# Strassen's block products for the up projections of a gated block on one Trainium2 core

## What is computed

```python
x = x + tanh(g_xattn[0]) * wkv(time_decay, time_first, k=layernorm(x), v=ctx_2048)
n = layernorm(x)
up_gate = einsum('bsd,hd->bsh', n, W1)      # W1, W3: 2048 x 512
up_lin  = einsum('bsd,hd->bsh', n, W3)
hidden  = fwht(silu(up_gate) * up_lin)      # Walsh-Hadamard along 2048, over sqrt(2048)
x = x + tanh(g_ffn[0]) * einsum('bsh,dh->bsd', hidden, W2)
```

## Time and profile before

| | us |
|---|---|
| median of 3 runs (range) | 1097.14 (1094.07 to 1098.11) |
| profiled execution | 1094.78 |
| its span, first to last instruction | 1093.0 |
| PE busy | 1060.4 |
| DVE, ACT, POOL busy | 585.2, 306.8, 290.7 |
| one steady run, from one store of the output to the next | 127.76 |
| mean granted TensorE clock | 0.997 |

### The profile page before, as it was taken

How to read it: one execution, slowest core, us unless ns; L and a number is a source line. 1 busy time by engine, 2 the same in 40 slices (tenths; PEclk the granted TensorE clock), 3 DMA queues, 4 the chain that set the end, 5 groups by cost and what they waited for, 6 DMA issues and landing times.

```text
span 1093.0 us, 12943 instructions
## 1 busy us (share of the span) xinstructions
PE 1060.4 (97%) x4878; PEld 498.6 (46%) x4972; DVE 585.2 (54%) x841; ACT 306.8 (28%) x377; POOL 290.7 (27%) x198
## 2 busy tenths in 40 slices
PE   5798999999999999999999999999999999999998
PEld 2365444444444444444444444444444444444443
DVE  7857986475284644665554752746436645531112
ACT  6756511413123311324113131143113241100000
POOL 0131152124321252223421244122521234211111
PEclk9899999999999999999999999999999999999999
DMA  9943030001200020001100012000200000000001
GB/s 351 345 182 130 1 116 1 40 1 38 77 1 40 24 93 1 3 39 39 77 1 39 1 39 77 3 39 7 109 1 1 39 1 1 1 39 1 1 1 39
DMA packets 19955, 55.65 MB, mean 51 GB/s; under 512 B 1072, under 2 KB 10416, under 8 KB 17072
## 3 DMA queue, kind: packets, MB, share of 16 engines
q1 hardware_dynamic: 19888, 54.73, 13.9%
HBM read 42.14 MB, written 12.58 MB: 50 GB/s over the span
## 4 chain that ended last, share of the span: by engine, by line
PE 90%; DVE 4%; ACT 2%; DMA 2%; issue 1%; SPq 1%; POOL 0%; DVEq 0%; ACTq 0%
PE pg L470 10%; PE po L478 10%; PE pl L470 10%; PE pg L468 10%; PE po L476 10%; PE pl L468 10%; PE pl L469 9%; PE po L477 9%; PE pg L469 9%; PE pst L403 1%; PE po L451 1%; DMA w_turn<-x 1%; DMA x<-w_t 1%; PE pst L434 1%; PE pst L439 1%
## 5 line engine op out<-in xcount | busy, mean ns | idle before, releaser
L1065 POOL TENSOR_TENSOR work<-work 128x512 bf16<-128x512 f32 (+1 forms) x132 | 202.4, 1533 | 700.2 <-DVE work L933 700.2
L926 DVE TENSOR_TENSOR work<-work,pl 128x512 f32<-128x512 f32 (+1 forms) x132 | 88.3, 669 | 429.1 <-PE pl L470 426.5
L649 ACT ACTIVATE work<-pg 128x512 f32<-128x512 f32 (+1 forms) x132 | 77.2, 584 | 610.3 <-PE pg L470 610.1
L468 PE MATMUL pg<-xn,w1h 128*128 128x512 f16 (+1 forms) x528 | 197.1, 373 | 3.3 <-ACT work L649 3.0
L470 PE MATMUL pg<-xn,w1l 128*128 128x512 f16 (+1 forms) x528 | 197.0, 373 | 1.8
L470 PE MATMUL pl<-xn,w3l 128*128 128x512 f16 (+1 forms) x528 | 196.7, 373 | 1.4
L468 PE MATMUL pl<-xn,w3h 128*128 128x512 f16 (+1 forms) x528 | 196.7, 373 | 0.0
L478 PE MATMUL po<-work,w 128*128 128x512 f16 x512 | 194.0, 379 | 1.7
L476 PE MATMUL po<-work,w 128*128 128x512 f16 x512 | 194.0, 379 | 0.0
L469 PE MATMUL pl<-xn,w3h 128*128 128x512 bf16 (+1 forms) x502 | 186.9, 372 | 0.0
L469 PE MATMUL pg<-xn,w1h 128*128 128x512 bf16 (+1 forms) x493 | 183.8, 373 | 0.0
(11 more groups left out here) (141 smaller groups left out, 892.5 us busy)
## 6 DMA issues: line engine op xcount, KB each, us to landing
ev<-ctx_t SPq DMA_DIRECT2D x7, 1024.0 KB, 5.7
xin<-x_t SPq DMA_DIRECT2D x7, 1024.0 KB, 5.0
bv<-x_tok SPq DMA_DIRECT2D x7, 1024.0 KB, 7.6
out_t<-x SPq DMA_DIRECT2D x7, 1024.0 KB, 3.9
x<-w_t SPq DMA_DIRECT2D x6, 512.0 KB, 6.5
w_turn<-work SPq DMA_DIRECT2D x2, 1024.0 KB, 7.3
xn<-w_t SPq DMA_DIRECT2D x4, 512.0 KB, 5.4
psum<-w_t SPq DMA_DIRECT2D x3, 512.0 KB, 10.0
```

What stands on the lines that cost most here:

```text
L468: pe.matmul(bank[:, 0:run.n(j)], hi, nh, start=(k == 0), stop=False)
L649: act.activation(sg[:, j % 2, 0:run.n(j)], pg[:, 0:run.n(j)], ACT.Silu).then_inc(gated, 1)
L926: dve.tensor_tensor(hf[:, j % 2, run.cols(j)], sg[:, j % 2, 0:n], pl[:, j % 2, 0:n], ALU.mult).then_inc(hidden, 1)
L1065: pool.tensor_tensor(hl[:, j % HBUF, run.cols(j)], hf[:, j % 2, run.cols(j)], hh[:, j % HBUF, run.cols(j)], ALU.subtract).then_inc(hid_lo, 1)
```

## The change

Runs 2 to 8 go by 8 pairs of slots. For a pair, the normalised chunk is four blocks (two halves of the 512 channels by the two batches), and so are the weights (two halves of the channels by the two slots of 128 rows). The four result blocks come from seven block products instead of eight, `part(run, p, i, w, ...)`: 6 matmuls of 256 columns for each of the weights W1 (w=0) and W3 (w=1). Products 1, 5, 6, 2, 7, 3, 4 are added up in halves of the banks: `chain` (first halves of `pg` and of the second `pl`), `fifth` (their second halves) and `second` (the other `pl`). ACT copies intermediate sums out (`keep_first`, `keep_sixth`), DVE adds them to the banks (`join`, six a pair), then come silu, the hidden products and clamps in three parts. Down products of a pair run inside the next one: high parts of slot 1, of slot 0, and last the low ones.

Four sums of activation blocks are made per chunk on DVE (`sum_blocks`) and split as the plain ones are; xn of a chunk moves from two passes of `norm_lo` to `plain_lo` and `sums_lo`. Four sums of weight blocks per unit are made on POOL (`weight_sums`) in run 1 and pairs 0 to 2 of run 2, from weights that are loaded a second time, cast on DVE (`wsum_hi_of`), split on POOL (`weight_sums_lo`) and stored to DRAM (`put_sums`), as the plain parts are (`put_plain`). Each pair's weights, 2 MB, are then read from there (`load_pair`), into a ring of two places; the load for pair p + 2 waits for product 4 of pair p.

The first norm of chunks 2 to 7 (the fronts of runs 2 to 7) no longer goes over PE: its factors are stored to DRAM and spread over the partitions (`spread_factors`), DVE scales the transposed input (`scale`), and ACT takes exps in place (`exps_in_place`). The front's DVE steps stand before and between the joins of pairs 0 to 7.

The core of the diff (indentation reduced; removed lines and blank ones left out):

```diff
+WEIGHTS_OF = {1: (0, 0, 0), 2: (0, 2, 0), 3: (0, 2, 1), 4: (1, 2, 0), 5: (1, 0, 0), 6: (1, 2, 1), 7: (1, 0, 1)}
+SUM_OF = {5: 0, 6: 1, 7: 2, 3: 3}
...
+def load_again(n):
+    if n < TRAWS:
+        sp.wait_ge(lin, Run(1).tile(1))
+        sp.wait_ge(plain_put[0], 16)
+    else:
+        sp.wait_ge(wsum_lo, n - TRAWS + 1)
+    w, p = units[n]
+    sp.dma_start(traw[n % TRAWS], raw_in[w][p]).then_inc(traw_loaded[n % TRAWS], 16)
...
+def put_sums(n):
+    w, p = units[n]
+    sp.wait_ge(wsum_lo, n + 1)
+    cols = slice(kind_of[w] * KT * PW, kind_of[w] * KT * PW + half_piece)
+    sp.dma_start(stage[p][:, 1, cols], tout[n % 2]).then_inc(sums_put[n % 2], 16)
...
+def load_pair(run, p):
+    if run.is_front(2) and p < 2:
+        sp.wait_ge(lin, Run(1).tile(11 if p == 0 else 15))
+        sp.wait_ge(plain_put[4 + 2 * p], 16)
+        sp.wait_ge(plain_put[5 + 2 * p], 16)
+    else:
+        sp.wait_ge(product[4][1], run.pair(p) - 1)
+    if run.is_front(2) and p < PAIRS:
+        sp.wait_ge(plain_put[p], 16)
+        for i in range(2):
+            sp.wait_ge(sums_put[i], 16 * (p + 1))
+    place = RING + 2 * (p % 2)
+    sp.dma_start(wts[:, place:place + 2, :, :, :].rearrange("p s a k n -> p s (a k n)"),
+                 stage[p % PAIRS]).then_inc(ring_loaded[p % 2], 16)
...
+def spread_factors(run):
+    sp.wait_ge(tok_chain, run.nth(0, 1) * TOK_STEPS)
+    if run.is_front(3):
+        sp.wait_ge(lin, Run(1).tile(5))
+        sp.wait_ge(plain_put[2], 16)
+    else:
+        sp.wait_ge(shifted, run.nth_rows(-1, NB))
+    sp.dma_start(factor_rows.rearrange("q (b p) -> p q b", p=P), tiny[:, 2:4, :],
+                 allow_slow_non_contiguous=True).then_inc(factors_put, 16)
+    sp.wait_ge(factors_put, run.nth_rows(0, 1) * 16)
+    sp.dma_start(token_rows.rearrange("p q n -> p (q n)"),
+                 factor_rows.rearrange("q n -> (q n)").partition_broadcast(P)).then_inc(factors_spread, 16)
...
+def steady(run, more=True, last=False):
+    for p in range(PAIRS):
+        if p == 1:
+            store(run.r - 2, 1 - run.par)
+        if p == 3 and more:
+            load_v(run.r + 1)
+        if p == 4 and more:
+            load_x(run.r + 1)
+            load_tokens(run.r + 1)
+        if p == 5 and more:
+            spread_factors(front_of(front_of(run)))
+        if run.is_front(2):
+            for n in {0: (8, 9), 1: (10, 11), 2: (12, 13), 3: (14, 15)}.get(p, ()):
+                put_sums(n)
+                if n + TRAWS < UNITS:
+                    load_again(n + TRAWS)
+        if not last or p + 2 < PAIRS:
+            load_pair(run, p + 2)
 load_half_tokens(0)
 sp.dma_start(mats[:, :], mats_in).then_inc(mats_loaded, 16)
...
+def part(run, p, i, w, bank, start, stop):
+    for k in range(2):
+        hi, lo = weights(p, i, w, k)
+        ah, al = operand(run, i, k)
+        pe.matmul(bank, hi, ah, start=(start and k == 0), stop=False, skip_group_check=True)
+        pe.matmul(bank, hi, al, start=False, stop=False, skip_group_check=True)
+        mm = pe.matmul(bank, lo, ah, start=False, stop=(stop and k == 1), skip_group_check=True)
+    return mm
...
+def pair(run, p, front):
+    g = run.pair(p)
+    begun = run.is_front(2) and p == 0
+    pe.wait_ge(ring_loaded[p % 2], (run.r * (PAIRS // 2) + (p // 2 + 1 - PAIRS)) * 16)
+    if p == 0:
+        pe.wait_ge(blocks_lo, run.nth_full(1, 4))
+    if begun:
+        pe.wait_ge(gated, Run(1).tile(SLOTS - 1))
+        pe.wait_ge(hidden, Run(1).tile(SLOTS - 1))
+    else:
+        pe.wait_ge(acted, g * 4)
+    part(run, p, 1, 0, chain[0], True, False)
+    part(run, p, 5, 0, fifth[0], False, False).then_inc(product[5][0], 1)
+    if not begun:
+        pe.wait_ge(pair_hidden, g * 3)
+    part(run, p, 1, 1, chain[1], True, False)
+    part(run, p, 5, 1, fifth[1], False, False).then_inc(product[5][1], 1)
+    if begun:
+        pe.wait_ge(hid_hi, Run(1).tile(SLOTS - 1))
+    else:
+        pe.wait_ge(pair_hi, g * 2 - 1)
+    high_downs(run, p, 1)
+    for w in range(2):
+        pe.wait_ge(kept1, g * 2 + (1 + w))
+        part(run, p, 6, w, chain[w], False, False).then_inc(product[6][w], 1)
+    part(run, p, 2, 0, second[0], True, True)
+    part(run, p, 2, 1, second[1], False, True).then_inc(product[2][1], 1)
+    if p == 0:
+        pe.wait_ge(blocks_lo, run.nth_full(3, 4))
+    for w in range(2):
+        pe.wait_ge(kept6, g * 2 + (1 + w))
+        part(run, p, 7, w, chain[w], False, False).then_inc(product[7][w], 1)
+    if not begun:
+        pe.wait_ge(pair_hi, g * 2)
+    high_downs(run, p, 0)
+    if front and p == 4:
+        mean_full(front_of(run))
+    if front and p == 5:
+        var_full(front_of(run))
+    for w in range(2):
+        pe.wait_ge(joined, g * 6 + (3 + w))
+        part(run, p, 3, w, fifth[w], False, True)
+        part(run, p, 4, w, chain[w], False, True).then_inc(product[4][w], 1)
+    if begun:
+        pe.wait_ge(hid_lo, Run(1).tile(SLOTS - 1))
+    else:
+        pe.wait_ge(pair_lo, g * 2)
+    low_downs(p, pair_down)
...
+def exps_in_place(run):
+    act.wait_ge(shifted, run.nth_rows(1, NB))
+    for k in range(KT):
+        act.activation(channel_rows(ea, run, k), channel_rows(ea, run, k), ACT.Exp,
+                       bias=bias[:, k:k + 1]).then_inc(exp_a, 1)
...
+def pair_silu(run, p, of, slot, b):
+    g, cols = run.pair(p), slice(b * T, b * T + T)
+    src = sg[:, slot, cols]
+    act.wait_ge(joined, g * 6 + of)
+    if (slot, b) == (0, 1):
+        act.wait_ge(product[4][0], g + 1)
+        if run.is_front(2) and p == 0:
+            act.wait_ge(hidden, Run(1).tile(SLOTS - 1))
+        else:
+            act.wait_ge(pair_hidden, g * 3)
+        src = chain[0]
+    act.activation(sg[:, slot, cols], src, ACT.Silu).then_inc(acted, 1)
+def pairs(run, front=True):
+    ahead = front_of(run)
+    for p in range(PAIRS):
+        keep_first(run, p)
+        keep_sixth(run, p)
+        if front and p == 0:
+            exps_in_place(ahead)
+        if front and p == 2:
+            logs(ahead)
+            inverses(ahead)
+        if front and p == 5:
+            squares(ahead)
+        if front and p == 7:
+            sums_hi(ahead, 0)
+            sums_hi(ahead, 1)
+            plain_hi(ahead, 1)
+        pair_silu(run, p, 1, 0, 0)
+        pair_silu(run, p, 3, 1, 1)
+        pair_silu(run, p, 5, 1, 0)
+        pair_silu(run, p, 5, 0, 1)
+        if front and p == 6:
+            blocks_ready(ahead)
+            plain_hi(ahead, 0)
 a, b = Run(0), Run(1)
...
+def scale(run):
+    dve.wait_ge(x_loaded, run.r * 16 - 16)
+    dve.wait_ge(factors_spread, run.nth_rows(0, 1) * 16)
+    dve.wait_ge(blocks_lo, run.nth_full(-1, 4))
+    for b in range(NB):
+        factor = token_rows[:, 0, b * T:(b + 1) * T].unsqueeze(1).to_broadcast([P, KT, T])
+        dve.tensor_tensor(batch_rows(ea, b), batch_cols(xin, b), factor, ALU.mult).then_inc(scaled, 1)
+    for b in range(NB):
+        dve.wait_ge(scaled, run.nth_rows(b, NB))
+        shift = token_rows[:, 1, b * T:(b + 1) * T].unsqueeze(1).to_broadcast([P, KT, T])
+        dve.tensor_tensor(batch_rows(ea, b), batch_rows(ea, b), shift, ALU.add).then_inc(shifted, 1)
...
+def sum_blocks(run):
+    a11, a12, a21, a22 = (plain_rows(k0, b) for b in range(NB) for k0 in (0, 2))
+    s1, s2, s3, s4 = (sum_rows(i) for i in range(TERMS))
+    dve.wait_ge(normed, run.nth_full(1, NB))
+    dve.tensor_tensor(s1, a21, a22, ALU.add).then_inc(xsum, 1)
+    dve.wait_ge(xsum, run.nth_full(0, TERMS))
+    dve.tensor_tensor(s2, s1, a11, ALU.subtract).then_inc(xsum, 1)
+    dve.tensor_tensor(s3, a11, a21, ALU.subtract).then_inc(xsum, 1)
+    dve.wait_ge(xsum, run.nth_full(1, TERMS))
+    dve.tensor_tensor(s4, a12, s2, ALU.subtract).then_inc(xsum, 1)
...
+def wsum_hi_of(n):
+    dve.wait_ge(wsum, TERMS * n + TERMS)
+    if n < 2:
+        dve.wait_ge(lin, Run(1).tile(3))
+        dve.wait_ge(plain_put[1], 16)
+    else:
+        dve.wait_ge(sums_put[n % 2], 16 * (n // 2))
+    dve.tensor_scalar(tout[n % 2][:, 0:KT * PW], traw[n % TRAWS], F16_MAX, -F16_MAX, ALU.min,
+                      ALU.max).then_inc(wsum_hi, 1)
...
+def pairs(run, front=True, more=True):
     ahead = front_of(run)
...
+    for p in range(PAIRS):
+        g = run.pair(p)
+        begun = run.is_front(2) and p == 0
+        if p == 1:
             for d in range(KT):
...
+                finish(run.r - 2, 1 - run.par, d, pair_down, run.pair(0) * KT + (d + 1))
+        if front and p == 0:
+            scale(ahead)
+        if front and p == 1:
+            scan(ahead, ea, eb, scan_b)
+        if front and p == 2:
+            with_token(ahead, ea, eb, scan_b, den_done, range(2, 4))
+            scan(ahead, v, bv, scan_a)
+        if front and p == 3:
+            with_token(ahead, v, bv, scan_a, num_done, range(2, 4))
+            over(ahead)
+            over_last(ahead, 0)
+        if front and p == 4:
+            residual(ahead)
+        if front and p == 5:
+            centre(ahead)
+            if more:
```

(92 more changed lines are left out.)

497 lines of the change are left out of this document (331 added, 166 removed).

## The result

Changed kernel: 1140.4 us, median of 4 runs (1137.4 to 1148.5). Before, in the same runs: 1097.3. Ratio 1.041 (95% 1.035 to 1.047), so 43 us slower, where 21 were forecast: the sign of the likeliest case, near the upper end of the range (1144). The profiled execution took 1142.9, its span is 1141.0.

A forecast was written before the change was run, and what follows sets the result against it. PE was taken as the bound, busy 1060.4 of 1093.0 us. Span 1093.0 - 77.0 + 63 (steady stalls) + 1.4 (finish and tail) + 35.5 (ramp) = 1116, plus 1.8 around it: 1118 us against 1094.8; range 1066 to 1144.

The forecast's parts named there:

- the likeliest case: Whole kernel: 98 to 150 us of stalls, time 1093 to 1148, chance 0.54; slower was given 0.51.
- PE's saving, 77: PE: 66.6 us less from 56 pairs at 14.35, and 10.6 from transposes of six fronts.
- Steady stalls, 63: Pairs of the six runs with a front: PE waits 10.5 us a run, 63 in all (29 to 68).
- pair 3: POOL's quotient and DVE's `over` and `over_last` shut each other out, delaying product 7's join: PE stalls 3.4 us.
- the rule that the prediction set beside its rows: DVE and POOL exclude each other at the port, tiny steps too: pair 5's stall 3.2 us, 2.5 taken.
- The ramp, 35.5: Run 1 and pairs 0 to 2 after it: 15, 2.5 and 18 us added, together 35.5 (10 to 58).
- wait before pair 0 of run 2: End of run 1: three low parts between the last hidden tile and pair 0 cost 2.5 us (1.5 to 4).
- Rival D: TensorE's clock falls with the new gaps and half-width matmuls cost 0.216 us; chance 0.02.
- The ring, 0: Pair weight loads: 2 MB in at most 15.2 us against 16.1; factors' round trip ahead of pair 7's load costs 0.
- rival B: Ring late: 2 MB loads over 16.1 us delay each of 56 pairs; at 18 us, 1180; chance 0.05.
- the signs named ahead: Among them: PE busy near 985 us, idle 100 or more; `out` stores 127 apart; ramp's pairs 0 to 2 at 20.
- the two signs that were to make it wrong: Steady runs of 118 us, or a ring load that ends a wait of PE.

The follow-up runs named there:

- Kernel 4: Changed kernel with `over` moved behind the joins of pair 3, `over_last` to pair 4 and the mean's matmul behind product 4: 1113.3 us (1.016).
- kernel 3: Changed kernel with run 1's variance, rsqrt and normalising a slot earlier, next moments a slot later, ACT's block-sum casts behind the next silu: 1131.0 us.
- kernel 10: Changed kernel without POOL's four sums and low part per unit; second loads, DVE's casts and stores stay, with wrong values: 1089.5 us.
- Kernel 1: Changed kernel without the weight sums, their second loads, casts and low parts; plain parts stored twice instead, so factors are wrong: 1088.2 us (0.993).
- kernel 2: Changed kernel with DVE's two casts in pairs 0 to 2 of the first paired run parted, and POOL's work with them: 1135.2 us.
- run 6: No follow-up: a stretch of eight pairs inside the kernel's execution, one of the six with a front; no separate length given.
- Run 8: No follow-up: the kernel's last stretch of pairs, without a front; its finish and uncovered tail were forecast at 1.4 us; pair 1 measured 15.09.

## Why the prediction was right and wrong

**PE's saving, 77: right.** Every pair that waits for nothing takes 14.35 us, to the hundredth.

**Steady stalls, 63: the mechanism of most parts was right, the sum by luck.** Per run, beyond 14.35 and the 0.86s: pair 1 0.8 (forecast 1.5), pair 2 1.04 (1.0), pair 3 2.8 (3.4), pair 5 2.35 (2.5), pair 6 1.03 (2.0), the rest 0: 8.0 against 10.5. The six runs with a front (2 to 7, run 2 from pair 3 on with the 1.8 of a steady run's pairs 0 to 2) lose 62.1 in all, against 63: 48 of these, 6.6 of half clock, 1.8 of the ring, 3.7 at the end of run 4 and the start of run 5, and 2 scattered. So the parts that were forecast gave 48 and not 63, and 14 that were not forecast made up for it. The 3.7 (3 to 4 in every version) lie where the loop over runs 3 and 4, then 5 and 6, jumps back. PE's branch at 630.58 takes 3.34 us in the trace (0.08 at 888.54, where the loop ends), PE stands 0.94 us at 634.38 for nothing that the profile shows, and DVE stands 5.3 us before an instruction that follows at once in every other steady run:

```profile
640.34 2.36 DVE L1175 TENSOR_TENSOR ev<-xin,wts 128x1024 f32<-128x1024 f32 x2 [5.26 <-issue]
```

No run here leaves the loop out, so the 3.7 as its price isn't tested. The prediction took all six runs as alike.

Pair 3 went as foretold. DVE, POOL and PE in run 3, where the pair starts at 425.42:

```profile
430.04 2.28 DVE L1222 TENSOR_TENSOR eb<-eb,ev 128x2048 f32<-128x2048 f32 x1
434.20 2.99 DVE L1234 SCALAR_TENSOR_TENSOR bv<-eb,bv 128x1024 f32<-128x1024 f32 x1 [1.88 <-POOL bv L1556]
```

```profile
430.20 5.91 POOL L1556 TENSOR_TENSOR bv<-bv,ev 128x1024 f32<-128x1024 f32 x2 [0.63 <-DVE bv L1215]
```

```profile
438.25 0.28 PE L721 MATMUL pg<-wts 128*128 128x256 f16 x1 [2.62 <-DVE work L1400]
438.37 0.27 PE L722 MATMUL pg<-wts 128*128 128x256 bf16 x1
...
439.30 0.42 PE L721 MATMUL pg<-xn,wts 128*128 128x256 f16 x1
439.51 0.42 PE L722 MATMUL pg<-xn,wts 128*128 128x256 bf16 x1
```

POOL's quotients begin under `over` and last 5.91 instead of 3.92; `over_last` waits for half 0, then for half 1 inside its own 2.99 us (1.21 when free), and PE stands 2.62 us. Kernel 4 took this order apart, and the wait went in every steady run: shown.

Pair 5 shows the rule that the prediction set beside its rows, and for 4-wide steps. DVE and POOL:

```profile
467.58 0.16 DVE L1127 SCALAR_TENSOR_TENSOR tiny<-tiny 128x4 f32<-128x4 f32 x1
467.78 1.89 DVE L1130 SCALAR_TENSOR_TENSOR tiny<-tiny 128x4 f32<-128x4 f32 x1
```

```profile
467.65 2.00 POOL L1546 TENSOR_TENSOR psum<-ev 128x1024 f32<-128x1024 f32 x1 [5.12 <-ACT ev L906]
```

A step of 0.16 us takes 1.89 beside POOL's sum. The exclusive lock of the Trainium skill ("SBUF — State Buffer", "Who interferes with whom") holds in this trace down to 4 elements a partition. The stall is 2.35, though, nearer to the 2.5 taken than to the 3.2 worked out by the rule.

**The ramp, 35.5: wrong by 26.5, and this is the step that failed.** By its terms, from starts of PE's instructions in the two kernels:

| | forecast | measured |
|---|---|---|
| run 1 up to slot 4 (95.17, 99.45) | 0 | 4.3 |
| slots 4 to 11, to the mean's matmul (156.75, 179.91) | 15 for run 1 | 18.9 |
| slots 12 to 15, to their end (192.24, 217.16) | | 1.7 |
| wait before pair 0 of run 2 | 2.5 | 12.8 |
| pairs 0 to 2 (44.9 in a steady run, 69.2) | 18 | 24.3 |
| sum | 35.5 | 62.0 |

It is over the upper end, 58, of its own range. The 4.3 up to slot 4 need not be the change's: kernel 3, the same program up to there, starts slot 4 at 95.23. The step that failed is the size of this term, and in it most of all the wait before pair 0, put at 2.5 and measured 12.8. I had counted three low parts between the last hidden tile and pair 0. For run 1 the sum priced POOL's work for units 0 to 4 alone; run 1 makes ten units, and those of slots 9 to 15 were put at nothing. But DVE's whole list from `rsqrt` on lies ahead of that pair, it runs beside these units, and it had slipped behind PE. DVE, then PE:

```profile
212.51 0.68 DVE L1315 TENSOR_TENSOR work<-work,pl 128x512 f32<-128x512 f32 x1
...
222.86 0.69 DVE L1315 TENSOR_TENSOR work<-work,pl 128x512 f32<-128x512 f32 x1 [2.18 <-issue]
...
226.71 4.27 DVE L1307 TENSOR_TENSOR wts<-ev,wts 128x1024 bf16<-128x1024 f32 x2
```

```profile
229.94 0.37 PE L721 MATMUL pg<-xn,wts 128*128 128x256 f16 x1 [12.78 <-DVE wts L1307]
```

The normalisation ends at 212.5; before, it ended 6.3 us ahead of pair 0's matmul, here 17.4 ahead. Between lie the sums of token blocks (new; 6.5 us, and 3.5 in kernel 10), the last hidden tile, for whose silu DVE stands 2.2 us, since ACT has casts of the block sums ahead of it, a cast, and low parts at 4.27 us for two (2.35 in kernel 10). The list of DVE was never laid out from `rsqrt` to pair 0, as it was for the eight steady pairs. Kernel 1 has 4.9 us there without the weight sums, so the block sums and low parts alone are twice the 2.5; the weight sums bring the other 7.9 (6.6 against kernel 10, which keeps their casts). Kernel 3's edit took off at most 4.7.

The rest of run 1 and pairs 0 to 2 went as foretold at 1.4 times the size, inside their ranges: in slots 4 to 11 mostly by POOL's turns at the port (the 15 us under kernel 10), in pairs 0 to 2 mostly by DVE's standing for POOL between two casts, 5.3 us a pair as against the 5.1 forecast. That it is POOL's part of the sums is shown by kernels 1 and 10, and the part with two casts by kernel 2. Without the weight sums (kernel 1) 13 of the 62 us are left: 3.7 up to slot 4, 1.5 from there to the end of run 1, 4.9 before pair 0 and 2.7 in pairs 0 to 2.

**The clock, not priced.** Rival D had it fall for good; it falls in spells. In the ramp the clock is 0.88, so (1 - 0.88) x 230 = 28 us at most, and about 16 by the spacing of matmuls (0.216 instead of 0.109), the rest lies in waits. In the steady runs it is four spells of 3.4 us at 1.2 instead of 2.4 GHz, three behind the wait of pair 3 and one in pair 5 of run 6: in pair 3 above, matmuls of 256 columns stand 0.12 apart after the wait of 2.62 and 0.21 apart from 439.30 on, and the pair takes 18.85 instead of 17.2. So the ramp's 62 hold some 16 of clock, and without it the forecast of the ramp would have been 10 short. That the spells go with the waits is shown for the steady runs by kernel 4 (1.00 with pair 3's wait gone). A wait is not enough, though: pair 3 has the same one in runs 6 and 7, without a spell. How much of the ramp's spells the waits bring on was only argued.

**The ring, 0: nearly right (1.8), by luck.** 2 MB land in 8.1 us, far from the 16.1 of rival B. But the slack I gave pair 7's load, a whole pair, wasn't there: the round trip of the factors takes 11 us in SP's queue ahead of it, and what is left is 9.1 against 8.1. The step priced the load and not the wait that it is queued behind.

**The rest.** Run 8: 0.7 (forecast 1.4). The sum with the measured terms is 1093.0 - 77.0 + 62.1 + 0.7 + 62.0 = 1140.8, and the span is 1141.0. Of the signs named ahead two fail: PE's busy time is 1023.8, not 985 (16 + 6.6 of these 39 us are half-clock matmuls, the rest I didn't trace), and pairs 0 to 2 are at 23, not 20. And one of the two signs that were to make it wrong is there in small, a load of the ring that ends a wait of PE: three times, 1.8 us in all.

## What to carry to other kernels

When work for POOL goes beside DVE, price each POOL instruction at the port, also against DVE's smallest steps, count all the units that a stretch makes, and lay out the whole list of DVE at every change of phase, not in the steady pairs alone. A load queued behind a round trip has the slack that the trip leaves. Behind a stall of PE look for a half-clock spell in the profile: removing the stall can give back both (in kernel 4 pair 3 gave back 20.9 us, 5.0 of them at half clock).

## What the runs showed of the hardware

- A DVE instruction of 4 elements a partition waits for a whole POOL instruction: 1.89 us instead of 0.16 beside a sum of 2.00.
- Of two engines at the port, the one that waits gets the turn between two instructions of the other: a POOL sum of 0.73 us took 2.60 between DVE's scans. So a string of small POOL sums and a string of DVE work go one by one.
- TensorE fell to half speed (1.2 GHz, from 0.11 to 0.21 us a matmul) 0.9 us after a wait of 2.62 us ended (1.0 and 0.0 in runs 4 and 5), for 3.4 us. The last wait before that one was of 0.88 us, 13 us earlier. In runs 6 and 7 the same wait had no such spell behind it.
- At the jump back of a loop PE's branch took 3.34 us in the trace and DVE stood idle for 5.3 us, with no semaphore or DMA that the profile shows.
- Slot 4 of run 1 starts at 99.45 us in after and at 95.23 in kernel 3, which is like it up to there, and the first half-clock spells lie elsewhere too; at the mean's matmul the two are 6.0 apart. So 4 to 6 us between two single runs of this kernel say nothing of an edit.
